# A graph layer on one core: more picks on the matrix engine, their index row read from PSUM, and a finer last group

## Chip, core and metric

The kernel runs on one NeuronCore of one Trainium2 chip. The metric is the device time of one execution in microseconds (us). The engines are named as in the profile: PE is TensorE (PEld its weight loads), DVE VectorE, ACT ScalarE, POOL GpSimd, SP the engine that only issues transfers here. Engines run their own streams and meet at semaphores.

## What is computed

The layer is a message-passing step of a graph network, with a residual and a layer norm behind it. 1,250 nodes have 128 features each, 20,000 edges have 50 features, a source, a destination (edges are sorted by destination) and a length.

```python
C = 0.5 * (cos(edge_length * (PI / CUTOFF)) + 1.0)
C = C * ((edge_length <= CUTOFF) & (edge_length >= 0.0))
h = gelu(edge_attr @ f_w0 + f_b0)
h = gelu(h @ f_w1 + f_b1)
h = gelu(h @ f_w2 + f_b2)
h = gelu(h @ f_w3 + f_b3)
xf = x @ lin1_w
msg = xf[src] * (h * C[:, None])
agg = segment_sum(msg, dst, num_segments=1250)
out = gelu(agg @ lin2_w + lin2_b) @ lin_w + lin_b
return layernorm(x + out)
```

## The kernel before

**Tiling.** The 20,000 edges are 160 tiles of 125; four tiles are a group (500 edges), two groups a pair, an even and an odd one. 20 pairs pass through a software pipeline. Nodes lie in ten chunks of 128. A loop over `passes` surrounds it all; for these inputs it runs once.

**The edge network.** PE makes layers 1 to 4 (`layer1` to `layer4`), ACT the gelus between them, and DVE adds the bias of layer 4 from PSUM (`add_bias4`, L666). Step p of the pipeline (function `pair` on each engine) makes layer 4 of pair p-1, layers 2 and 3 of pair p, layer 1 of pair p+1, and the messages and the scatter of pair p-2. Below, "the pair" of a message is q = p-2.

**Source rows.** `xf` is computed once (L433), copied from PSUM by ACT (L328) and written to DRAM. POOL then fetches `xf[src]` with one indirect DMA for each tile (L310), 125 rows of 512 bytes, in a fixed order, into eight slots of `gathered`. The gathers of a group wait only until the group eight before has been read. The two groups of pair 0 take another way (raw rows of x, L294, L493, L500).

**Picks.** For some pairs POOL leaves out the last tile of the odd group, and the rows are picked instead: DVE compares the tile's source numbers with the node numbers (`build_pick`, L710; ten chunks by 125 columns, a 0/1 matrix in bf16), PE multiplies this with `xf` split in three bf16 parts (`pick_rows`, L509, ten matmuls into bank `ps_pick`), and DVE sums the three parts into the free slot (L697). Before, this is done in 14 pairs (q mod 4 is 0, 1 or 2, without pair 0). The source numbers are broadcast to all 128 rows by a DMA from DRAM (875 KB) and cast by DVE (L729).

**Messages and scatter.** DVE builds the weighted one-hot of destinations (L675 hit, L677 onehot; both inputs in SBUF), multiplies h by the gathered rows (`message`, L682), and PE scatters four tiles of a group into a 64-column window (`scatter`, L483), which DVE adds to `aggT` (L719). A scatter waits for its whole group's message.

**End.** After the last scatter come `lin2` (L576), a gelu (ACT, L337), `lin` (L583) onto bias and residual that PE has put into PSUM earlier (`add_residual`, L516, L519), and the layer norm in three pieces of two, four and four chunks: statistics and the roots, then normalising on DVE (pieces 0 and 2, L776) and ACT (piece 1, L417), and the stores.

## Time and profile before

| what | value |
|---|---|
| median of 3 runs | 257.4 us (257.32 to 258.51) |
| profiled execution, its own time | 258.03 us |
| span from first to last instruction in it | 256.2 us |
| mean granted TensorE clock | 0.933 of 2.4 GHz |
| PE busy | 223.5 us (87%), 1130 instructions |
| DVE busy | 135.1 us (53%), 252 instructions |
| ACT busy | 110.0 us (43%), 181 instructions |
| POOL busy | 191.1 us (75%), 155 instructions |

The profile is of one execution; times in it count from its first instruction. "Busy" of POOL is the time in its gathers; between two of them the profile shows about 0.3 us of "issue", in which nothing is waited for. The profiled execution took 0.6 us more than the median.

### The profile page before, as it was taken

How to read it: one execution, taken by the hardware profiler on the slowest of the kernel's cores; microseconds unless marked ns; L12 is line 12 of the kernel's file. 1: busy time of each engine (PE TensorE's matmuls, PEld its weight loads, DVE VectorE, ACT ScalarE, POOL GpSimd, SP SyncE). 2: the span in 40 equal slices, each digit the busy share in tenths (PEclk: the TensorE clock that was granted, in tenths of full speed). 3: DMA queues.
4: the chain of work that ended last, by engine and by line, in shares of the span. 5: the costliest groups of instructions: out<-in, count | busy, mean ns of one | idle time of the engine just before them, and what ended most of it. 6: DMA issues, size and time to landing. Idle time of an engine off the chain costs nothing.

```text
span 256.2 us, 3892 instructions
## 1 busy us (share of the span) xinstructions
PE 223.5 (87%) x1130; PEld 148.6 (58%) x1130; DVE 135.1 (53%) x252; ACT 110.0 (43%) x181; POOL 191.1 (75%) x155
## 2 busy tenths in 40 slices
PE   3889999999799999899999599979968997898480
PEld 3535676765666766666766367555626565675350
DVE  5682186553666653666655356644424575613135
ACT  2457655354455364455365334515352453100052
POOL 6887888888888878888877888888778788887000
PEclk9999999999999999999999979989997999955587
DMA  6862222221221221221221212212121211111003
GB/s 209 248 202 72 75 74 46 70 75 46 66 72 42 70 74 41 72 72 41 69 75 41 75 37 72 72 36 72 47 72 40 72 31 43 41 45 45 10 0 101
DMA packets 17904, 17.70 MB, mean 69 GB/s; under 512 B 9244, under 2 KB 15183, under 8 KB 17894
## 3 DMA queue, kind: packets, MB, share of 16 engines
q0 software_dynamic: 11296, 9.52, 15.4%
q1 hardware_dynamic: 5872, 7.48, 9.6%
q10 hardware_dynamic: 726, 0.59, 0.8%
q8 instruction: 4, 0.07, 0.1%
q14 instruction: 6, 0.05, 0.0%
HBM read 16.14 MB, written 1.28 MB: 68 GB/s over the span
## 4 chain that ended last, share of the span: by engine, by line
POOL 53%; PE 21%; issue 15%; DVE 3%; ACT 2%; DMA 1%; POOLq 1%; ACTq 1%; another core or an unknown queue 1%; DVEq 1%
POOL gathered L310 53%; PE ps_agg L483 3%; PE ps_even L470 3%; PE ps_even L457 2%; PE ps_even L448 2%; PE ps_odd L457 2%; PE ps_even L462 2%; PE ps_odd L462 2%; PE ps_pick L509 1%; PE ps_odd L470 1%; DMA gathered<-xf_dram,src_idx 1%; PE ps_even L576 1%; DVE stats L762 1%; PE ps_odd L576 1%
## 5 line engine op out<-in xcount | busy, mean ns | idle before, releaser
L310 POOL DMA_INDIRECT gathered<-xf_dram,src_idx x138 | 180.4, 1307 | 42.1 <-issue 41.1
L483 PEld LDWEIGHTS ps_agg<-onehot,messages 125*128 125x128 f32 x320 | 43.8, 204 | 38.8 <-DVE messages L682 22.2
L483 PE MATMUL ps_agg<-onehot,messages 125*128 125x64 f32 x320 | 45.0, 287 | 17.8 <-DVE messages L682 15.9
L337 ACT ACTIVATE h<-ps_odd,biases_sb 128x500 f32<-128x500 f32 x61 | 41.3, 677 | 34.0 <-PE ps_odd L462 14.4
L337 ACT ACTIVATE h<-ps_even,biases_sb 128x500 f32<-128x500 f32 x61 | 40.9, 670 | 21.4 <-PE ps_even L462 9.7
L335 ACT ACTIVATE h<-pre 125x512 f32<-125x512 f32 x40 | 25.0, 626 | 51.8 <-DVE pre L666 43.4
L682 DVE TENSOR_TENSOR messages<-h,gathered 125x512 f32<-125x512 f32 x38 | 26.1, 690 | 32.5 <-DMA gathered<-xf_dram,src_idx 30.7
L470 PEld LDWEIGHTS ps_odd<-w_mlp_sb,h 128*125 128x125 f32 x160 | 21.3, 194 | 9.8 <-issue 9.8
L509 PE MATMUL ps_pick<-xf_parts,pick 128*125 128x384 bf16 x140 | 25.7, 331 | 0.0
L666 DVE TENSOR_TENSOR pre<-ps_odd,row_b_sb 125x512 f32<-125x512 f32 x20 | 13.8, 692 | 22.4 <-PE ps_odd L470 17.9
L509 PEld LDWEIGHTS ps_pick<-xf_parts,pick 128*125 128x125 bf16 x140 | 18.0, 136 | 12.5 <-issue 9.6
L457 PE MATMUL ps_even<-h,w_mlp_sb 128*128 128x500 f32 x40 | 23.0, 659 | 2.1 <-ACT h L337 2.1
L448 PE MATMUL ps_even<-edge_in,w_mlp_sb 50*128 50x500 f32 x42 | 24.1, 654 | 0.1
L470 PE MATMUL ps_even<-w_mlp_sb,h 128*125 128x128 f32 x160 | 24.1, 298 | 0.0
L448 PE MATMUL ps_odd<-edge_in,w_mlp_sb 50*128 50x500 f32 x42 | 24.1, 654 | 0.0
L666 DVE TENSOR_TENSOR pre<-ps_even,row_b_sb 125x512 f32<-125x512 f32 x20 | 13.8, 692 | 15.4 <-issue 10.6
L470 PEld LDWEIGHTS ps_even<-w_mlp_sb,h 128*125 128x125 f32 x160 | 21.0, 204 | 1.6 <-ACT h L337 1.6
L470 PE MATMUL ps_odd<-w_mlp_sb,h 128*125 128x128 f32 x160 | 21.3, 277 | 0.0
L462 PE MATMUL ps_odd<-h,w_mlp_sb 128*128 128x500 f32 x40 | 21.0, 607 | 0.0
L719 DVE TENSOR_TENSOR aggT<-aggT,ps_agg 128x64 f32 x40 | 8.9, 222 | 22.7 <-PE ps_agg L483 16.4
L457 PE MATMUL ps_odd<-h,w_mlp_sb 128*128 128x500 f32 x40 | 20.7, 599 | 0.0
L462 PE MATMUL ps_even<-h,w_mlp_sb 128*128 128x500 f32 x40 | 20.6, 595 | 0.0
(107 smaller groups left out, 184.5 us busy)
## 6 DMA issues: line engine op xcount, KB each, us to landing
edge_in<-in_edge_attrT SPq DMA_DIRECT2D x44, 97.7 KB
gathered<-xf_dram,src_idx POOLq DMA_INDIRECT x138
picked_i<-in_picked_src SPq DMA_DIRECT2D x1, 875.0 KB
xf_dram<-xf_sb SPq DMA_DIRECT2D x2, 256.0 KB
lin_xT_sb<-in_lin_xT SPq DMA_DIRECT2D x1, 369.0 KB
lin_xT_sb<-in_lin_xT SPq DMA_DIRECT2D x1, 320.0 KB, 3.1
w_mlp_sb<-in_w_mlp ACTq DMA_DIRECT2D x1, 256.0 KB
out<-normed SPq DMA_DIRECT2D x1, 256.0 KB
```

The costliest lines, as they stand in the source:

```text
L310: nc.gpsimd.indirect_dma_start(out=gathered[0:TILE, b, t, :], out_offset=None, in_=xf_dram[:, :], in_offset=bass.IndirectOffsetOnAxis(ap=s ...
L335: nc.scalar.activation(out_ap, in_ap, GELU).then_inc(done, 1)
L337: nc.scalar.activation(out_ap, in_ap, GELU, bias=biases_sb[:, layer:layer + 1]).then_inc(done, 1)
L448: nc.tensor.matmul(ps1[b][:, 0:GROUP], w0[b], edge_in[rows, slot, :], start=True, stop=True).then_inc(l1_done, 1)
L457: nc.tensor.matmul(ps23[b][:, 0:GROUP], w_mlp_sb[:, 1, :], h1[:, b, :], start=True, stop=True).then_inc(l2_done, 1)
L462: nc.tensor.matmul(ps23[b][:, 0:GROUP], w_mlp_sb[:, 2, :], h2[:, b, :], start=True, stop=True).then_inc(l3_done, 1)
L470: last = nc.tensor.matmul(ps4[b][0:TILE, t * FEAT:(t + 1) * FEAT], h3[:, b, t * TILE:(t + 1) * TILE], w_mlp_sb[:, 3, :], start=True, stop= ...
L483: last = nc.tensor.matmul(ps_agg[:, b * WINDOW:(b + 1) * WINDOW], messages[:, slot, t, :], onehot[:, p % 2, b * TILES_PER_GROUP + t, :], s ...
L509: last = nc.tensor.matmul(ps_pick[0:TILE, 0:3 * FEAT], pick[:, c, :], xf_parts[:, c, :, :].rearrange("p a f -> p (a f)"), start=(c == 0), ...
L666: nc.vector.tensor_tensor(pre4[:, (2 * p + b) % 4, :, :], ps4[b][0:TILE, :].rearrange("p (t f) -> p t f", f=FEAT), row_b3_sb[:, :].rearran ...
L682: nc.vector.tensor_tensor(messages[:, slot, :, :], h4[:, slot, :, :], rows_of_x, ALU.mult)\
L719: nc.vector.tensor_tensor(window, window, ps_agg[:, b * WINDOW:(b + 1) * WINDOW], ALU.add).then_inc(agg_added, 1)
```

## The change

1. A pick is made in every pair from 1 to 18 (18 picks instead of 14), so POOL issues 134 gathers instead of 138. The last pair has none.
2. The source numbers of the picks are no longer broadcast by DMA: one row of 9 KB is loaded on ACT's queue. For each pick PE spreads its 125 numbers over all partitions with a matmul of one row (`spread_pick_row`, `ones` x `picked_f`) into columns 384 to 508 of `ps_pick`, and DVE compares from there.
3. The split of `xf` in three parts is made from the PSUM banks, where the product still lies, instead of from its SBUF copy, in twelve smaller instructions, and stands earlier in DVE's order. PE waits for it ahead of the first layer 3.
4. ACT runs a gelu of one column behind the copies of `xf`, which brings the table load forward.
5. The very last group has a semaphore for each tile: four messages of a tile each, and each matmul of its scatter waits for its own.
6. The last four node chunks lie in two banks (`ps4[1]` and `ps_pick`), and their normalising is shared by DVE (two chunks) and ACT (two chunks).

Core of the diff:

```diff
-PICKED = (0, 1, 2)
+PICKS = PAIRS - 2
 def gathers_of(g):
-    return TILES_PER_GROUP - (g % 2 and is_picked(g // 2))
+    return TILES_PER_GROUP - (g % 2 and 0 < g // 2 < PAIRS - 1)
...
-            sp.wait_ge(xf_stored, 64)
-            sp.dma_start(picked_i[:, :, :].rearrange("p k e -> p (k e)"), picked_src.to_broadcast((ROWS, PICKS * TILE)))\
-                .then_inc(picked_loaded, 16)
...
+            act.dma_start(picked_i[:, :], picked_src).then_inc(picked_loaded, 16)
...
+            nc.scalar.activation(std[0:TILE, 0:1], half_pi[:, 0:1], GELU)
...
-                def pick_rows(before, turn, p):
-                    pe.wait_ge(parts_ready, 1)
-                    pe.wait_ge(pick_ready, r * PICKS + turn * len(PICKED) + picks_through(p))
+                def spread_pick_row(before, turn, p):
+                    pe.wait_ge(picked_cast, 1)
                     pe.wait_ge(message_done, before * (2 * TURN_PAIRS) + (2 * p + message_credit))
+                    nc.tensor.matmul(ps_pick[:, 3 * FEAT:3 * FEAT + TILE], ones[0:1, :],
+                                     picked_f[0:1, bass.ds(turn * (TURN_PAIRS * TILE) + (p - 1) * TILE, TILE)],
+                                     start=True, stop=True).then_inc(pick_row_done, 1)
+
+                def pick_rows(turn, p):
+                    pe.wait_ge(pick_ready, r * PICKS + turn * TURN_PAIRS + p)
...
                     layer3(before, p, 1)
                     if p >= 2:
+                        spread_pick_row(before, turn, p - 1)
                         scatter(before, p - 2, 1)
...
+                pe.wait_ge(parts_ready, 1)
                 layer3(first, 0, 0)
...
-                scatter(last, 3, 1)
+                scatter(last, 3, 1, by_tile=True)
...
+                def message_last(before):
+                    for t in range(TILES_PER_GROUP):
+                        if t == 0:
+                            dve.wait_ge(act4_done, before * (2 * TURN_PAIRS) + 2 * TURN_PAIRS)
+                        dve.wait_ge(last_landed[t], r * 16 + 16)
+                        ins = nc.vector.tensor_tensor(messages[:, 3, t, :], h4[:, 3, t, :],
+                                                      gathered[0:TILE, GATHER_SLOTS - 1, t, :], ALU.mult)
...
                 def build_pick(turn, p):
-                    row = picked_f[:, bass.ds(turn * len(PICKED) + (picks_through(p) - 1), 1), :]\
+                    dve.wait_ge(pick_row_done, r * PICKS + turn * TURN_PAIRS + p)
+                    row = ps_pick[:, 3 * FEAT:3 * FEAT + TILE].rearrange("p (o e) -> p o e", o=1)\
                         .to_broadcast((ROWS, NODE_CHUNKS, TILE))
```

PE, second half of a pipeline step (layer 3, the scatter of both groups). Before:

```order
L509 MATMUL ps_pick<-xf_parts,pick 125x384 x10
L462 MATMUL ps_even<-h,w_mlp_sb 128x500
L480 REGISTER_ALU
L483 MATMUL ps_agg<-onehot,messages 128x64 x4
L462 MATMUL ps_odd<-h,w_mlp_sb 128x500
L480 REGISTER_ALU
L483 MATMUL ps_agg<-onehot,messages 128x64 x4
```

and now:

```order
L518 MATMUL ps_pick<-xf_parts,pick 125x384 x10
L461 MATMUL ps_even<-h,w_mlp_sb 128x500
L480 REGISTER_ALU
L487 MATMUL ps_agg<-onehot,messages 128x64 x4
L461 MATMUL ps_odd<-h,w_mlp_sb 128x500
L510 REGISTER_ALU
L511 MATMUL ps_pick<-picked_f,ones 128x125
L487 MATMUL ps_agg<-onehot,messages 128x64 x4
```

The spreading matmul L511 stands between layer 3 and the scatter of the odd group; it waits for the same message as that scatter did.

DVE, the messages of a pair that had no pick before (q mod 4 is 3; `hit` to the next pick matrix). Before:

```order
L675 TENSOR_TENSOR hit<-dst_rel,iota_f 125x512
L676 REGISTER_ALU
L677 REGISTER_ALU
L677 TENSOR_TENSOR onehot<-hit,cut 125x512
L682 TENSOR_TENSOR messages<-h,gathered 125x512 x2
L710 ISA
L710 TENSOR_TENSOR pick<-picked_f,node_ids 128x1250
```

and now:

```order
L698 TENSOR_TENSOR hit<-dst_rel,iota_f 125x512
L699 REGISTER_ALU
L700 REGISTER_ALU
L700 TENSOR_TENSOR onehot<-hit,cut 125x512
L705 TENSOR_TENSOR messages<-h,gathered 125x512
L724 TENSOR_REDUCE gathered<-ps_pick 125x128
L713 ISA
L705 TENSOR_TENSOR messages<-h,gathered 125x512
L745 REGISTER_ALU
L749 TENSOR_TENSOR pick<-ps_pick,node_ids 128x1250
```

The sum of the picked rows stands between the two messages, as it did in the other pairs, and the compare L749 takes its first input from `ps_pick`.

DVE at the start, around the number of passes. Before, the split (L651 to L654) stood behind the tables; now it stands ahead of them:

```order
L642 CAST passes_i<-passes_f 1x1
L649 CAST xf_parts<-ps_even 128x4x128
L649 CAST xf_parts<-ps_odd 128x4x128
L649 CAST xf_parts<-ps_pick 128x2x128
L652 TENSOR_TENSOR ps_even<-ps_even,xf_parts 128x512
L652 TENSOR_TENSOR ps_odd<-ps_odd,xf_parts 128x512
L652 TENSOR_TENSOR ps_pick<-ps_pick,xf_parts 128x256
```

Six more of this kind follow, then the tables of destinations and weights and the cast of the 2,250 source numbers on one partition.

## Rows read from the trace of the kernel before

**Rows 1.** The page, part 4: engines' shares of the chain that ended last.
```profile
POOL 53%; PE 21%; issue 15%; DVE 3%; ACT 2%; DMA 1%; POOLq 1%; ACTq 1%; another core or an unknown queue 1%; DVEq 1%
```

**Rows 2.** Group of the gathers by line: xcount | busy us, mean ns | idle before <-releasers.
```profile
L310 POOL DMA_INDIRECT gathered<-xf_dram,src_idx x138 | 180.4, 1307 | 42.1 <-issue 41.1 <-DVE messages L682 0.9
```

**Rows 3.** Stretches: length, busy PE PEld DVE ACT POOL, PEclk, DMA share, GB/s.
```profile
66.00:134.00 68.00, 67.06 (x374) 45.33 (x374) 41.78 (x68) 34.13 (x56) 55.23 (x42) 1.00 0.24 61
134.00:220.00 86.00, 76.33 (x391) 50.46 (x391) 44.14 (x72) 35.56 (x59) 69.85 (x54) 0.94 0.21 54
226.00:246.00 20.00, 15.07 (x49) 11.28 (x49) 4.26 (x9) 0.83 (x2) 8.75 (x8) 0.51 0.11 28
246.00:253.00 7.00, 2.79 (x22) 2.35 (x20) 5.29 (x30) 4.58 (x10) 0.00 (x0) 0.96 0.02 7
```

**Rows 4.** Timeline (start, length, engine, line, tiles [idle before]): the first two and the last gather.
```profile
14.76 2.31 POOL L310 DMA_INDIRECT gathered<-xf_dram,src_idx  x1 [0.30 <-issue]
17.37 1.96 POOL L310 DMA_INDIRECT gathered<-xf_dram,src_idx  x1 [0.30 <-issue]
...
235.68 1.20 POOL L310 DMA_INDIRECT gathered<-xf_dram,src_idx  x1 [0.30 <-issue]
239.19 0.69 DVE L682 TENSOR_TENSOR messages<-h,gathered 125x512 f32<-125x512 f32 x1 [5.44 <-DMA gathered<-xf_dram,src_idx]
```

**Rows 5.** Timeline: a gather that starts inside a pick's compare.
```profile
205.04 1.46 DVE L710 TENSOR_TENSOR pick<-picked_f,node_ids 128x1250 bf16<-128x1250 f32 x1
205.11 2.45 POOL L310 DMA_INDIRECT gathered<-xf_dram,src_idx  x1 [0.30 <-issue]
```

**Rows 6.** Timeline: gathers that start inside other DVE products, PSUM or SBUF input.
```profile
34.52 0.69 DVE L682 TENSOR_TENSOR messages<-h,ps_agg 125x512 f32<-125x512 f32 x1 [0.97 <-PE ps_agg L500]
34.93 1.19 POOL L310 DMA_INDIRECT gathered<-xf_dram,src_idx  x1 [0.30 <-issue]
...
110.10 0.68 DVE L675 TENSOR_TENSOR hit<-dst_rel,iota_f 125x512 f32 x1
...
110.39 1.47 POOL L310 DMA_INDIRECT gathered<-xf_dram,src_idx  x1 [0.30 <-issue]
```

**Rows 7.** Timeline: three odd messages (pairs 6, 8, 9), PE between the last two.
```profile
94.95 0.69 DVE L682 TENSOR_TENSOR messages<-h,gathered 125x512 f32<-125x512 f32 x1 [0.28 <-DVE gathered L697]
...
113.98 0.69 DVE L682 TENSOR_TENSOR messages<-h,gathered 125x512 f32<-125x512 f32 x1 [0.27 <-DVE gathered L697]
...
116.36 1.09 PE L470 MATMUL ps_even<-w_mlp_sb,h 128*125 128x128 f32 x8
...
120.97 1.84 PE L509 MATMUL ps_pick<-xf_parts,pick 128*125 128x384 bf16 x10
...
123.60 0.69 DVE L682 TENSOR_TENSOR messages<-h,gathered 125x512 f32<-125x512 f32 x1 [0.19 <-DVE gathered L697]
```

**Rows 8.** Timeline: the start.
```profile
11.95 1.28 ACT L337 ACT_TABLE_LOAD   x1 [2.44 <-issue]
...
16.76 1.49 DVE L654 TENSOR_TENSOR xf_parts<-xf_rest,xf_parts 128x1280 bf16<-128x1280 f32 x1
...
18.36 1.10 PE L462 MATMUL ps_even<-h,w_mlp_sb 128*128 128x500 f32 x2
```

**Rows 9.** Timeline: the end, PE, ACT and DVE.
```profile
217.45 1.09 PE L470 MATMUL ps_even<-w_mlp_sb,h 128*125 128x128 f32 x8
...
220.96 0.69 PE L516 MATMUL ps_odd<-row_lin_b_sb,ones 1*128 1x256 f32 x2
...
239.94 1.97 PE L483 MATMUL ps_agg<-onehot,messages 125*128 125x64 f32 x8 [4.16 <-DVE messages L682]
...
242.67 1.22 PE L576 MATMUL ps_even<-aggT,w_node_sb 128*128 128x256 f32 x2 [0.76 <-DVE aggT L719]
...
246.59 0.69 ACT L337 ACTIVATE nodeT<-ps_even,biases_sb 128x512 f32<-128x512 f32 x1 [0.26 <-PE ps_even L576]
...
252.02 1.36 DVE L776 TENSOR_SCALAR normed<-ps_odd,mean_var,rstd 128x128 f32<-128x128 f32 x4
```

More of the change, by code:

```diff
@@ L420, in _ @@
             root(2)
-            act.wait_ge(normed_done[2], 1)
+            act.wait_ge(shift_done, 2)
+            c0, c1 = pieces[2]
+            for c in range((c0 + c1) // 2, c1):
+                last = nc.scalar.activation(normed[:, c, :], out_rows_of(c),
+                                            ACT.Identity, bias=shift[:, c:c + 1], scale=rstd[:, c:c + 1])
+            last.then_inc(normed_done[2], 1)
+            act.wait_ge(normed_done[2], 2)
             act.dma_start(out[FULL_CHUNKS * ROWS:NODES, :], normed[0:REST, FULL_CHUNKS, :]).then_inc(out_stored, 16)
@@ L582, in lin @@
                 for c in range(c0, c1):
[L583 removed]
+                    last = nc.tensor.matmul(out_rows_of(c),
                                             nodeT[:, c * ROWS:(c + 1) * ROWS], w_node_sb[:, 1, :],
[L585 removed]
+                                            start=False, stop=(c + 1 in [half[1] for half in halves]))
                 last.then_inc(node3_done, 1)
@@ L631, in _ @@
             nc.vector.tensor_copy(passes_i[:, :], passes_f[:, :]).then_inc(passes_ready, 1)
+            dve.wait_ge(xf_copied, 3)
+            xf_whole = [xf_bank[k][:, 0:(c1 - c0) * FEAT].rearrange("p (c f) -> p c f", f=FEAT)
+                        for k, (c0, c1) in enumerate(chunk_cuts)]
+            parts = [[xf_parts[:, c0:c1, part, :] for c0, c1 in chunk_cuts] for part in range(3)]
+            for k in range(3):
+                last = nc.vector.tensor_copy(parts[0][k], xf_whole[k])
+            chain(last)
+            for k in range(3):
+                last = nc.vector.tensor_tensor(xf_whole[k], xf_whole[k], parts[0][k], ALU.subtract)
+            chain(last)
+            for k in range(3):
+                last = nc.vector.tensor_copy(parts[1][k], xf_whole[k])
+            chain(last)
+            for k in range(3):
+                last = nc.vector.tensor_tensor(parts[2][k], xf_whole[k], parts[1][k], ALU.subtract)
+            last.then_inc(parts_ready, 1)
             chain(nc.vector.tensor_tensor(
@@ L790, in _ @@
             invert(2)
+            negate_mean(2)
             normalise(2)
```

132 lines of the change are left out of this document (68 added, 64 removed).

## The prediction, made before the changed kernel was run

> **What bounds the kernel now.** I read the chain that ended last first: over half of the span is POOL's gathers, and "issue", most of which stands between two gathers, is 15% [rows 1]. So the reader should see one engine that issues transfers from the beginning to the end. The groups by line then give the price of a gather: 138 gathers, 180.4 us busy and 42.1 us idle before them, of which only 0.9 us is a wait for a message [rows 2]. An undisturbed gather takes 1.19 us [rows 6]; with 42.1 / 138 = 0.305 us between two, the step is 1.495 us. At 1.19 us each, 138 gathers would be 164.2 us busy; the other 16.2 us is lengthening. With it POOL's time closes: the first gather starts at 14.76, 137 steps are 204.8, and 14.76 + 204.8 + 16.2 = 235.8, against 235.68 where the last one starts; its message starts 3.5 us later, at 239.19 [rows 4]. I call that moment T.
>
> PE is the second bound. From 66 to 134 us it is busy 67.06 of 68 us, from 134 to 220 only 76.33 of 86 [rows 3]: until about 134 the pairs run at PE's pace, then at POOL's. From one odd message to the next a PE-paced pair with a pick takes 123.60 - 113.98 = 9.6 us, 9.7 on average over several such pairs [rows 7]. Seven gathers take 7 x 1.495 = 10.5 us, so POOL, which has a head start, is slowly overtaken.
>
> **What lengthens a gather.** Rows 5 and 6 belong together. A gather that starts 0.07 us into a pick's compare takes 2.45 us: it ends 1.06 us after the compare [rows 5]. One that starts inside `hit`, which has two SBUF inputs, takes 1.47 us and ends 1.08 us after it; one that starts inside a message whose second input lies in PSUM takes 1.19 us, nothing more [rows 6]. I looked at each of the 138 in this way: 14 meet a compare and lose 10.4 us together, the first two meet the split of `xf` and lose 1.12 + 0.77 = 1.9 us [rows 4], 15 others lose 3.5 us together, a few tenths each, to `hit`, `onehot`, messages and a cast. Only the start of a gather is sensitive: a compare that begins 0.13 us or more after it costs nothing.
>
> The Trainium skill, page "SBUF — State Buffer", section "Summary: rules for kernel authors", says that a DVE instruction with two SBUF inputs contends with a GpSimd instruction that reads SBUF, and one with at most one SBUF input does not; the rows above agree. The same section also says, as inferred, that `tensor_tensor` does not stall descriptor generation, since that needs the write interface. By that sentence the compare's second input would not be what delays a gather, and moving it to PSUM would give nothing; the 2.45 us speaks against it, but I keep it as a rival (rival D).
>
> **The change part by part, at T.**
> (a) Four gathers less: 4 x 1.495 = 6.0 us off POOL's time.
> (b) The compare takes its row from PSUM, as the message at 34.52 did. The 10.4 us of 14 picks go, and the 18 picks cost POOL nothing. Bounds: all 10.4, or, if the delay stays, 10.4 / 14 x 18 = 13.4 in their place. I take the first, because rows 6 show the same kind of instruction at the same moment of a gather.
> (c) The split works from PSUM and is over before; its 1.9 us go. But the tables (of which some have two SBUF inputs) and a cast of 2,250 numbers now come behind it, at about 17 to 21 us, among the first gathers. Between 0 and 2 us; I take 1.0, since a cast of some 1.4 us covers the start of one gather almost surely.
> (d) The other meetings. Pair by pair `hit` and `onehot` cover 1.37 us of each 1.495 us step, so about one gather in each pair starts inside one of them and loses 0 to 0.6 us, 0.3 on average; the two messages stand in the step at nearly the same phases (1.4 and 3.8 us behind `hit`), so that they seldom cost a second time. Until now the compare pushed the gathers aside in each pair and left 3.5 us of this; without it I take 17 x 0.27 = 4.5 us, 1.0 more. Bounds: 0, and 10.5 us if the four products meet gathers independently (0.68 / 1.495 x 0.34 = 0.155 us each, 4 x 17 of them).
> T moves by -6.0 - 10.4 - 1.9 + 1.0 + 1.0 = -16.3 us, from 239.2 to 222.9.
>
> **PE's side.** Each spread adds one fp32 matmul of 125 columns with one row. The nearest row is the bias row of 256 columns, 0.69 us busy with its latency [rows 9]; four matmuls of 128 columns take 1.09 us [rows 7], 0.27 each. So 0.2 to 0.6 us, and I take 0.25: 18 x 0.25 = 4.5 us. It adds no wait on PE: it waits for the odd message, and the scatter queued right behind it waits for the same. What is new is on DVE: the compare can't start until layer 3 and the spread are through, about 1 us later than now, and the window sums and the next bias stand behind it. PE needs the matrix 4.6 us after a step begins (120.97 - 116.36 [rows 7]), so the cover is about 3.8 us; the next bias starts some 0.4 us later and its gelu has more slack than that. The four new picks are 1.8 us of PE each, but a step without a pick doesn't save as much now: pairs 7 (unpicked) and 8 together take 113.98 - 94.95 = 19.0 us, only 0.4 less than two picked ones [rows 7]. So I add 0.4 us for each. The table load of 1.28 us goes from the path ahead of the first gelu [rows 8]; the new wait for the split before layer 3 (now at 18.36, the split ends at 18.25) takes some of it back: I take 0.8 gained, between 0 and 1.3.
> The odd message of pair 9 is now at 123.60; it moves to 123.60 - 0.8 (start) + 9 x 0.25 (spreads) + 2 x 0.4 (picks of pairs 3 and 7) = 125.9. Eight pairs of 9.95 later comes that of pair 17, at 205.5, and 2 us later the tail. At full clock it is two layers 4 (1.8), a pick (1.8), bias and residual of ten chunks (5.8, by 0.69 for a bias and 0.22 to 0.35 for a chunk) and three scatters (2.5), 11.9 us: PE is ready for the last group at 219.4, which is 3.5 us ahead of T. So POOL still sets the end, and PE sets the pace until shortly before it. If POOL lost nothing at all in (c) and (d), T would be 217.4, and PE would be the bound at 219.4.
>
> **Behind T.** Now 256.2 - 239.2 = 17.0 us.
> (e) Message, scatter and the wait behind it: now 3.5 us from T to the start of `lin2` at 242.67, with a scatter of 1.97 us at the low clock [rows 9]. Then a quarter message (0.2), one matmul (0.2 to 0.5), the two window sums (0.6) and latencies: 1.4. -2.1 us.
> (f) The clock. The granted clock was about half (1.2 GHz) from 226 to 246 us, and nearly full from 246 on [rows 3]; before it fell PE had been busy only part of the time, waiting for messages. `lin2` took 242.67 to 246.59, 3.9 us [rows 9]; at 2.4 GHz it would be some 2.2. With PE busy up to 219.4 the low clock may come later or not at all. Between 0 and -1.7 (and +1 if `lin` falls into it as well); I take -1.0.
> (g) Normalising the last four chunks is 1.36 us on DVE [rows 9]; two chunks are 0.7, ACT's two end about 0.3 later. -0.4 us.
> Bias and residual in two banks add one matmul, hidden ahead of T.
>
> **Sum.** 256.2 - 16.3 - 2.1 - 1.0 - 0.4 = 236.4 us span. The profiled execution was 1.8 us longer than its span and 0.6 above the median, so 236.4 + 1.2 = 237.6 us.
>
> **Rivals.**
> A, the forecast: POOL sets the end, PE the pace; 234 to 240 us. 0.53.
> B: the gathers meet DVE's remaining products independently, now that DVE follows PE's pace and no compare realigns them: 10.5 instead of 4.5 us, 237.6 + 6.0 = 243.6. For it: 18 steps in which the phase wanders. Against: only 3.5 us now. 0.16.
> C: PE becomes the bound. A spread costs 0.55 us and not 0.25 (its operand address is computed anew each time, and its weights are another tile): 219.4 + 18 x 0.3 = 224.8, 1.9 above T, but the clock is then high behind it: 237.6 + 1.9 - 0.7 = 238.8. 0.12.
> D: the compare delays gathers from PSUM, too. T is 222.9 + 13.4 = 236.3; 237.6 + 13.4 = 251. Against it: 34.93 [rows 6]. 0.05.
> E: hardly any meeting, and a tail at full clock: T at PE's 219.4, so -3.5, and -0.7: 233.4. 0.10.
> F, slower than before: a compare with a row repeated from PSUM runs far slower than the 1.46 us of now, in the loop PE (spread), DVE (compare), PE (pick). The cover decides: beyond 1.46 + 3.8 = 5.3 us every further us is on PE's path 18 times. At 6.7 us, 219.4 + 18 x 1.4 = 244.6 is 21.7 us over T: 259. Messages from PSUM take 0.69 us as those from SBUF do, which speaks against it; a repeated row from PSUM is in no row. 0.03. What remains (0.01) is no difference.
>
> **Range and chances.** The likeliest case gives 237.6. From B's 243.6 down to E's 233.4 lie A, B, C and E, over 0.9; PE's start gained in full (0.5 less) moves the lower end to 232.8, and I leave the range at 232.8 to 243.8. Differences under 0.5% are about what a measurement of this kernel can't tell from none. Faster by more than 0.5%: A to E, 0.96. Same 0.01, slower 0.03.
>
> **What the changed profile would show.** 134 gathers with a mean of 1.22 to 1.25 us (now 1.307); none that starts inside a compare above 1.3 us; the compare still near 1.46 us; the last gather starting at about 219.4, with its message 3.5 us later; PE over 95% busy up to 200 us and a full clock there; `lin2` starting 1.4 us behind the last tile's message. I would be wrong if gathers inside compares still take 2 us (D), if the mean is 1.27 or more (B), or if PE has no idle time ahead of the last scatter (C, F).

## The result and the profile after

| | before | after |
| --- | --- | --- |
| device time, median | 257.95 us (4 runs, 257.32 to 261.54) | 250.64 us (4 runs, 248.47 to 250.86) |
| span of the profiled execution | 256.2 us | 248.9 us (250.74 us of device time) |
| PE busy | 223.5 us (87%), 1130 matmul instructions | 232.5 us (93%), 1208 matmul instructions |
| POOL busy | 191.1 us (75%) | 176.4 us (71%) |
| mean granted clock of PE | 0.933 | 0.954 |

The ratio of the times is 0.9705, with a 95% interval of 0.9632 to 0.9779: the change makes the kernel 3% faster. The prediction was 237.6 us, in a range of 232.8 to 243.8. The sign was right, the time was not: it came out 13.0 us above the forecast and outside the range. In the span the miss is 248.9 - 236.4 = 12.5 us, and the rest of this text accounts for those. Some executions of all these kernels are some us longer throughout, whatever the kernel; the times given below are those of the others (261.54 in the table is a long one), and where only a long one was profiled, single distances are read from it.

The first line is the chain that ended last of the kernel after, as in [rows 1]: it was 53% POOL, and it is 93% PE now. Two groups follow from the view by lines, the gathers (as in [rows 2]) and the compare.

```profile
PE 93%; DVE 2%; issue 2%; DMA 2%; ACT 0%; SPq 0%; DVEq 0%
```

```profile
L299 POOL DMA_INDIRECT gathered<-xf_dram,src_idx x134 | 166.1, 1240 | 41.0 <-issue 39.2 <-DVE messages L705 1.8
L749 DVE TENSOR_TENSOR pick<-ps_pick,node_ids 128x1250 bf16<-128x1250 f32 x18 | 26.3, 1460 | 28.4 <-PE ps_pick L511 17.0 <-issue 11.4
```

134 gathers with a mean of 1240 ns (1307 before) and a compare that still takes 1460 ns: POOL's side is what the prediction said. The stretches of the kernel after, in the columns of [rows 3], show where the time went instead:

```profile
66.00:134.00 68.00, 68.00 (x374) 45.58 (x373) 41.30 (x66) 31.24 (x52) 54.58 (x45) 1.00 0.25 63
134.00:220.00 86.00, 86.00 (x472) 57.29 (x470) 54.31 (x87) 40.27 (x66) 68.92 (x57) 1.00 0.23 59
220.00:240.00 20.00, 19.23 (x70) 14.21 (x69) 5.08 (x16) 2.32 (x4) 1.08 (x1) 0.57 0.02 6
```

PE, the second number behind the length, is busy 68.00 of 68 and 86.00 of 86 us. In [rows 3] it was busy 76.33 of 86 in the second stretch. It has no idle time at all up to the end of the pairs, and then it works at 0.57 of its clock. (Busy means here that an instruction was in PE; rows that overlap count once, so it doesn't say how densely columns were streamed.) These are the end of POOL's work, PE in the tail and DVE in the tail, in three pieces of the timeline of the kernel after:

```profile
219.44 1.64 POOL L299 DMA_INDIRECT gathered<-xf_dram,src_idx  x1 [0.31 <-issue]
```

```profile
222.22 1.66 PE L528 MATMUL ps_even<-ident,lin_xT_sb 128*128 128x128 f32 x8
223.67 1.81 PE L487 MATMUL ps_agg<-onehot,messages 125*128 125x64 f32 x8
...
229.87 3.51 PE L487 MATMUL ps_agg<-onehot,messages 125*128 125x64 f32 x16
234.15 1.22 PE L585 MATMUL ps_even<-aggT,w_node_sb 128*128 128x256 f32 x2 [0.77 <-DVE aggT L758]
```

```profile
228.10 0.89 DVE L737 TENSOR_TENSOR messages<-h,gathered 125x128 f32<-125x128 f32 x4
233.52 0.58 DVE L758 TENSOR_TENSOR aggT<-aggT,ps_agg 128x64 f32 x2 [4.53 <-PE ps_agg L487]
```

The last gather starts at 219.44. PE reaches the last group's scatter (the second half of the 16 matmuls at 229.87) only at about 231.6, when all four of its messages (228.10) are long written: DVE waits 4.53 us for PE, and nobody waits for a gather. A scatter of eight matmuls takes 1.81 us at 223.67; the same one takes 1.0 us in the pairs.

### The profile page after: what moved, and what is told of

The parts are those of the page before. It is cut to its first block, busy times and chain, and to the rows that moved or that the text cites. A ratio compares the mean times of both kernels' runs of the same rounds, so it can differ in the third digit from the quotient of the medians.

```text
span 248.9 us, 4074 instructions
## 1 busy us (share of the span) xinstructions
PE 232.5 (93%) x1208; PEld 155.5 (62%) x1208; DVE 145.3 (58%) x270; ACT 111.0 (45%) x184; POOL 176.4 (71%) x151
## 4 chain that ended last, share of the span: by engine, by line
PE 93%; DVE 2%; issue 2%; DMA 2%; ACT 0%; SPq 0%; DVEq 0%
PE ps_agg L487 16%; PE ps_pick L518 13%; PE ps_even L447 9%; PE ps_even L469 7%; PE ps_odd L461 7%; PE ps_even L461 7%; PE ps_odd L469 7%; PE ps_even L456 7%; PE ps_odd L456 7%; PE ps_pick L511 3%; DMA lin_xT_sb<-in_lin_xT 2%; PE ps_even L585 1%; PE ps_even L432 1%; PE ps_odd L528 1%; PE ps_odd L525 1%
## 5 line engine op out<-in xcount | busy, mean ns | idle before, releaser
L299 POOL DMA_INDIRECT gathered<-xf_dram,src_idx x134 | 166.1, 1240 | 41.0 <-issue 39.2
L330 ACT ACTIVATE h<-ps_even,biases_sb 128x500 f32<-128x500 f32 x61 | 40.8, 669 | 28.3 <-issue 13.7
L487 PEld LDWEIGHTS ps_agg<-onehot,messages 125*128 125x128 f32 x320 | 42.7, 202 | 10.6 <-issue 8.4
L487 PE MATMUL ps_agg<-onehot,messages 125*128 125x64 f32 x320 | 44.4, 285 | 0.0
L749 DVE TENSOR_TENSOR pick<-ps_pick,node_ids 128x1250 bf16<-128x1250 f32 x18 | 26.3, 1460 | 28.4 <-PE ps_pick L511 17.0
L518 PEld LDWEIGHTS ps_pick<-xf_parts,pick 128*125 128x125 bf16 x180 | 23.1, 136 | 16.3 <-issue 12.6
L518 PE MATMUL ps_pick<-xf_parts,pick 128*125 128x384 bf16 x180 | 33.1, 331 | 0.0
L469 PEld LDWEIGHTS ps_odd<-w_mlp_sb,h 128*125 128x125 f32 x160 | 20.5, 188 | 8.7 <-issue 8.7
L461 PE MATMUL ps_even<-h,w_mlp_sb 128*128 128x500 f32 x40 | 21.0, 607 | 2.1 <-issue 2.1
L461 PE MATMUL ps_odd<-h,w_mlp_sb 128*128 128x500 f32 x40 | 21.9, 630 | 0.0
L469 PE MATMUL ps_even<-w_mlp_sb,h 128*125 128x128 f32 x160 | 21.9, 280 | 0.0
L456 PE MATMUL ps_even<-h,w_mlp_sb 128*128 128x500 f32 x40 | 20.2, 586 | 1.0 <-issue 1.0
L469 PE MATMUL ps_odd<-w_mlp_sb,h 128*125 128x128 f32 x160 | 20.7, 273 | 0.0
L469 PEld LDWEIGHTS ps_even<-w_mlp_sb,h 128*125 128x125 f32 x160 | 19.3, 189 | 1.8 <-issue 1.0
L724 DVE TENSOR_REDUCE gathered<-ps_pick 125x128 f32<-125x384 f32 x18 | 10.0, 557 | 15.6 <-PE ps_pick L518 9.9
```

The lines of the kernel that those rows point to most:

```text
L299: nc.gpsimd.indirect_dma_start(out=gathered[0:TILE, b, t, :], out_offset=None, in_=xf_dram[:, :], in_offset=bass.IndirectOffsetOnAxis(ap=s ...
L330: nc.scalar.activation(out_ap, in_ap, GELU, bias=biases_sb[:, layer:layer + 1]).then_inc(done, 1)
L456: nc.tensor.matmul(ps23[b][:, 0:GROUP], w_mlp_sb[:, 1, :], h1[:, b, :], start=True, stop=True).then_inc(l2_done, 1)
L461: nc.tensor.matmul(ps23[b][:, 0:GROUP], w_mlp_sb[:, 2, :], h2[:, b, :], start=True, stop=True).then_inc(l3_done, 1)
L469: last = nc.tensor.matmul(ps4[b][0:TILE, t * FEAT:(t + 1) * FEAT], h3[:, b, t * TILE:(t + 1) * TILE], w_mlp_sb[:, 3, :], start=True, stop= ...
L487: last = nc.tensor.matmul(ps_agg[:, b * WINDOW:(b + 1) * WINDOW], messages[:, slot, t, :], onehot[:, p % 2, b * TILES_PER_GROUP + t, :], s ...
```

## The experiments

The working theory after this trace had three parts. First, a spread costs PE 0.6 us and not 0.25, because its operands have one row and stand between matmuls with full operands. Second, PE's new wait for the split delays the start. Third, the tail runs at 1.2 GHz although PE is never idle in it. The rivals were that a spread costs so much by its place or its columns, that the compare in PSUM or its later start is what holds the pairs, and that gathers set the end after all.

### The spread with operands of 128 rows

The stationary operand `ones` and the moving one `picked_f` get 128 rows. All rows of `picked_f` but the first are zero, so the sum is the same.

```diff
-        ones = sb("ones", [GROUPS, ROWS])
+        ones = sb("ones", [ROWS, ROWS])
-        picked_f = sb("picked_f", [1, PICKS * TILE])
+        picked_f = sb("picked_f", [ROWS, PICKS * TILE])
...
-                    nc.tensor.matmul(ps_pick[:, 3 * FEAT:3 * FEAT + TILE], ones[0:1, :],
-                                     picked_f[0:1, bass.ds(...)],
+                    nc.tensor.matmul(ps_pick[:, 3 * FEAT:3 * FEAT + TILE], ones[:, :],
+                                     picked_f[:, bass.ds(...)],
...
+            chain(nc.vector.memset(picked_f[:, :], 0.0))
-            nc.vector.tensor_copy(picked_f[:, :], picked_i[:, :]).then_inc(picked_cast, 1)
+            nc.vector.tensor_copy(picked_f[0:1, :], picked_i[:, :]).then_inc(picked_cast, 1)
```

> The spreading matmul gets an operand of 128 rows (127 of them zero) instead of one row; everything else is the changed kernel. Theory S (a spread costs 0.61 us of PE's step, of which only some 0.2 us is its own columns, the rest the change between a one-row operand and full ones): the step falls from 10.31 to about 9.95 us, 18 x 0.36 = 6.5 us less, 244 to 245 us, PE still the bound. Rival (the cost is the wait for the message and the register work ahead of the spread, whatever its operand): step 10.3, 250.7 us.

Measured: 242.26 us (242.14 and 242.38), a ratio to before of 0.9386 (0.9281 to 0.9492), 8.4 us less than the changed kernel. PE around the spread, from the timeline, first of the changed kernel and then of this one:

```profile
109.86 1.06 PE L461 MATMUL ps_odd<-h,w_mlp_sb 128*128 128x500 f32 x2
110.85 0.48 PE L511 MATMUL ps_pick<-picked_f,ones 1*128 x2
111.26 1.10 PE L487 MATMUL ps_agg<-onehot,messages 125*128 125x64 f32 x8
112.20 1.09 PE L469 MATMUL ps_even<-w_mlp_sb,h 128*125 128x128 f32 x8
```

```profile
204.51 1.06 PE L461 MATMUL ps_odd<-h,w_mlp_sb 128*128 128x500 f32 x2
205.40 0.38 PE L511 MATMUL ps_pick<-picked_f,ones 128*128 x2
205.62 1.01 PE L487 MATMUL ps_agg<-onehot,messages 125*128 125x64 f32 x8
206.46 1.09 PE L469 MATMUL ps_even<-w_mlp_sb,h 128*125 128x128 f32 x8
```

The busy times overlap, so the reader should take starts. From the start of L461 to that of L469 it is 2.34 us with one row and 1.95 us with 128. The same stretch without a spread is 1.74 us in the trace of before:

```profile
114.62 1.06 PE L462 MATMUL ps_odd<-h,w_mlp_sb 128*128 128x500 f32 x2
115.52 1.00 PE L483 MATMUL ps_agg<-onehot,messages 125*128 125x64 f32 x8
116.36 1.09 PE L470 MATMUL ps_even<-w_mlp_sb,h 128*125 128x128 f32 x8
```

So a spread of one row costs 0.60 us and one of 128 rows 0.21 us. The other 0.39 us lies in the one-row matmul and on both sides of it: the one before it takes 0.99 instead of 0.89 us until the next starts, the spread 0.41 instead of 0.22, and the scatter behind it 0.94 instead of 0.84. The step from one odd message to the next goes from 10.31 to 9.92 us, on average over the 16 from pair 1 to pair 17. Over these 16 it is 6.2 us; another 2.3 us of the difference at pair 17 (212.21 against 203.78) was there at pair 1 already and comes from the start, which scatters (below). The expectation had the step right and the whole time 2 us too high, since it left out the start.

With this one edit the two bounds meet. POOL, PE and DVE at the end, from the timeline of this kernel:

```profile
220.44 1.20 POOL L299 DMA_INDIRECT gathered<-xf_dram,src_idx  x1 [0.30 <-issue]
```

```profile
221.33 3.52 PE L487 MATMUL ps_agg<-onehot,messages 125*128 125x64 f32 x16
223.74 0.29 DVE L738 TENSOR_TENSOR messages<-h,gathered 125x128 f32<-125x128 f32 x1 [1.12 <-DMA gathered<-xf_dram,src_idx]
```

The last tile's message waits for its gather and is written at 224.03. But PE doesn't wait for it: its 16 matmuls run without a pause, and the two of the last tile start at 224.2. So neither engine alone is the bound there; the chain that ended last is 59% PE and 21% POOL, whose gathers stand at its end. `lin2` starts at 225.97, 5.5 us behind the last gather's start. The forecast said 4.9.

### Every spread issued twice

If 0.2 us of the 0.6 are the spread's own columns and 0.4 the change of shape, then a second one of the same shape, right behind the first, must cost 0.2 us.

```diff
                                      start=True, stop=True)
+                    nc.tensor.matmul(ps_pick[:, 3 * FEAT:3 * FEAT + TILE], ones[0:1, :],
+                                     picked_f[0:1, bass.ds(...)], start=True, stop=True)
```

> Each spread is issued twice, one behind the other, into the same columns. Theory S: the second one costs its columns alone, 0.2 us, 18 x 0.2 = 3.7 us more, 254 to 255 us, step 10.5. Rival (each one-row matmul costs the whole 0.6 us): 11 us more, 261.7 us, step 10.9.

Measured: 249.55 us, in one execution; the expected 3.7 us more don't show in it. The profiled execution has a span of 254.9 us, so I read single starts from its timeline:

```profile
113.50 1.06 PE L461 MATMUL ps_odd<-h,w_mlp_sb 128*128 128x500 f32 x2
114.49 0.48 PE L511 MATMUL ps_pick<-picked_f,ones 1*128 x2
114.81 0.38 PE L514 MATMUL ps_pick<-picked_f,ones 1*128 x2
115.12 1.10 PE L487 MATMUL ps_agg<-onehot,messages 125*128 125x64 f32 x8
```

From L461 to L487 it is 1.62 us, where one spread takes 1.40 (109.86 to 111.26 above): the second costs 0.22 us, and the step grows by 0.22 us, to 10.53. That settles the split of the price, by the timeline and not by the whole time. What makes the switch dear was not separated further. The Trainium skill, page "TensorEngine Tiling (Array Packing)", section "Key Properties", says that changing the tiling mode drains TensorE; the extra time on both sides of the one-row matmul fits that. Whether a one-row operand is such a change, and the drain itself, no run here shows.

### The split of `xf` back behind the tables

The split works from the SBUF copy again, behind the tables, and PE's wait for it stands ahead of the first pick instead of ahead of the first layer 3.

```diff
                 next_layer1(first, 0)
-                pe.wait_ge(parts_ready, 1)
                 layer3(first, 0, 0)
...
+            dve.wait_ge(xf_copied, 3)
+            chain(nc.vector.tensor_copy(xf_parts[:, :, 0, :], xf_sb[:, :, :]))
+            chain(nc.vector.tensor_tensor(xf_rest[:, :, :], xf_sb[:, :, :], xf_parts[:, :, 0, :], ALU.subtract))
```

> The split of xf is made from its SBUF copy behind the tables again, PE waits for it only at the first pick. Theory W (PE's wait of 2.1 us for the split, and the stretch at 1.2 GHz behind it, cost 2 us of PE's path): the odd message of pair 1 comes at about 45.3 instead of 47.3 us, 248 to 249 us in all; the two first gathers lengthen again by some 2 us, which costs nothing as POOL isn't the bound. Rival (the end is set by POOL): 252 us.

Measured: 247.37 us (247.12 and 247.62), a ratio to before of 0.9584 (0.9475 to 0.9694). PE's start, from the timeline of the changed kernel, with the end of the split on DVE between, and then of this one:

```profile
12.68 1.10 PE L456 MATMUL ps_even<-h,w_mlp_sb 128*128 128x500 f32 x2 [1.01 <-issue]
...
17.31 0.41 DVE L658 TENSOR_TENSOR xf_parts<-ps_pick,xf_parts 128x256 bf16<-128x256 f32 x1
```

```profile
17.78 1.95 PE L461 MATMUL ps_even<-h,w_mlp_sb 128*128 128x500 f32 x2 [2.13 <-issue]
```

```profile
12.64 1.10 PE L457 MATMUL ps_even<-h,w_mlp_sb 128*128 128x500 f32 x2 [1.24 <-ACT h L331]
...
15.55 1.11 PE L462 MATMUL ps_even<-h,w_mlp_sb 128*128 128x500 f32 x2
```

Both start layer 2 at 12.6 to 12.7 us at the full clock. From there to layer 3 it is 5.10 us with the wait and 2.91 without: the wait costs 2.2 us. Behind it layer 3 takes 1.95 us instead of 1.11, since the granted clock fell just as the wait ended (at 17.9); until the next layer 4 this is another 1.4 us. The odd message of pair 1 came at 47.30 and comes at 43.66 now, 3.6 us earlier, and from pair 17 to the end both take the same 36.7 us. So all that this edit moves is the start, and by more than the expected 2 us, which had left out part of the low clock's price.

### The row broadcast by DMA and compared from SBUF

18 picks as in the changed kernel, but the source numbers come as before: broadcast, cast on all partitions, and the compare has two SBUF inputs. No spreads.

```diff
-                    row = ps_pick[:, 3 * FEAT:3 * FEAT + TILE].rearrange("p (o e) -> p o e", o=1)\
+                    row = picked_f[:, bass.ds(turn * TURN_PAIRS + (p - 1), 1), :]\
```

> 18 picks, but their source numbers are broadcast by DMA and compared from SBUF as before; no spreads. Theory (a compare with two SBUF inputs delays a gather by 0.74 us, one from PSUM does not): the gathers' mean rises from 1.240 to about 1.34 us, the last one starts at about 232 instead of 219.4, PE (11 us less to do) waits for it, 250 to 253 us in all. Rival (what delayed the gathers before was something else than the compare's second SBUF input): last gather at 220, PE bound at 240 us.

Measured: 250.02 us (249.12 and 250.93), a ratio of 0.9687 (0.9551 to 0.9824), as slow as the changed kernel, for another reason. The gathers by line, and a gather that starts inside a compare, from the timeline:

```profile
L303 POOL DMA_INDIRECT gathered<-xf_dram,src_idx x134 | 173.5, 1295 | 43.1 <-issue 42.2 <-DVE messages L698 0.9
```

```profile
209.59 1.46 DVE L741 TENSOR_TENSOR pick<-picked_f,node_ids 128x1250 bf16<-128x1250 f32 x1
...
209.98 2.14 POOL L303 DMA_INDIRECT gathered<-xf_dram,src_idx  x1 [0.30 <-issue]
```

The gather ends 1.07 us after the compare, as the one in [rows 5] did (1.06). The gathers are 7.4 us longer together than in the changed kernel, and the last one starts at 228.87 instead of 219.44. In the kernel with operands of 128 rows a gather that starts 0.71 us into a compare with its row in PSUM takes 1.18 us:

```profile
205.82 1.46 DVE L750 TENSOR_TENSOR pick<-ps_pick,node_ids 128x1250 bf16<-128x1250 f32 x1 [1.35 <-PE ps_pick L511]
206.53 1.18 POOL L299 DMA_INDIRECT gathered<-xf_dram,src_idx  x1 [0.30 <-issue]
```

This holds for all of them: of the 16 gathers that start inside a compare here, 15 end 1.05 to 1.07 us after it (the other starts at its very end), while none of the 18 in the changed kernel, nor of the 18 in the one with 128 rows, takes more than 1.20 us. So the compare's second SBUF input is what delays a gather, and not, as the inferred sentence behind rival D would have it, something else. The pairs give the spread's price once more: from pair 1 to pair 9 PE sets the pace here too, and a step takes 9.70 us without a spread against 10.31 with it, 0.61 us. The move to PSUM is worth its matmul, if that has full operands: this kernel without any spread is 7.8 us slower than the one with them (250.02 against 242.26).

### Useless matmuls in PE's tail

The changed kernel, with seven repetitions of a layer 2 product (500 columns, into a bank whose content nobody reads any more) among the tail's small matmuls.

```diff
+                def filler():
+                    nc.tensor.matmul(ps1[0][:, 0:GROUP], w_mlp_sb[:, 1, :], h1[:, 0, :], start=True, stop=True)
...
+                filler()
                 pick_rows(LAST_TURN, 2)
                 add_residual(0)
+                filler()
                 scatter(last, 2, 0)
                 add_residual(1)
+                filler()
                 scatter(last, 2, 1)
                 add_residual(2)
                 add_residual(3)
+                filler()
                 scatter(last, 3, 0)
+                filler()
                 scatter(last, 3, 1, by_tile=True)
```

Two more stand inside the last scatter.

> The changed kernel with seven matmuls more in PE's tail, each like layer 2 (500 columns, 128 rows) into a bank that nobody reads: work that does nothing. Theory K (PE, though never idle there, runs its last 11 us and lin2 at 1.2 GHz, which costs 5 to 8 us of the path, because what it does there is small): the granted clock stays high to the end of the scatter, 7 x 0.84 = 5.9 us more work, 5.3 + 2 us less, so 249 to 250 us, lin2 2.9 instead of 4.7 us long. Rival (the low clock comes at that place whatever PE does): 250.7 + 5.9 or, at the low clock, + 11.7, 257 to 262 us.

First the clock in the changed kernel's tail, in short stretches, and then in this kernel's, from its tail's start to `lin2` and through it (columns as in [rows 3]):

```profile
222.00:223.00 1.00, 1.00 (x6) 0.79 (x6) 0.00 (x0) 0.00 (x0) 0.00 (x0) 0.85 0.16 52
223.00:224.00 1.00, 1.00 (x8) 1.00 (x6) 0.00 (x0) 0.00 (x0) 0.00 (x0) 0.50 0.00 0
```

```profile
215.40:236.80 21.40, 20.68 (x112) 14.16 (x110) 9.83 (x21) 1.90 (x3) 5.80 (x5) 1.00 0.07 17
236.80:241.00 4.20, 4.16 (x24) 3.15 (x25) 1.11 (x6) 2.85 (x4) 0.00 (x0) 1.00 0.00 0
```

Measured: the clock stays at 2.4 GHz through the whole tail and `lin2`. In the changed kernel it falls to 1.2 GHz at 222.7, with PE busy 1.00 of 1.00 us during and after the fall. What PE does there are biases of one row, residual products of 128 columns with the identity, and scatters of 64 columns. The tail from its first layer 4 to `lin2` takes 19.58 us (217.26 to 236.84) against 18.87 (215.28 to 234.15), with 7 x 0.84 = 5.9 us of useless work in it: without that it would be 13.7, so the low clock costs 5.2 us there. From `lin2` to the end it is 12.0 instead of 14.75 us. From the odd message of pair 17 to the end it is 34.7 us instead of 36.7. The first row of `lin2` in this timeline (its like of the changed kernel, 1.22 us at 234.15, stands above):

```profile
236.84 0.70 PE L596 MATMUL ps_even<-aggT,w_node_sb 128*128 128x256 f32 x2 [0.76 <-DVE aggT L769]
```

In the whole time the 2.0 us don't show: 248.56 us (247.0 to 250.67), on another chip and without a ratio to before, and with an odd message of pair 1 at 48.59, 1.3 us later than in the changed kernel's trace. What is shown is the tail alone.

The other traces bear it out. In eight profiled executions with PE at or near the bound and no useless matmul in the tail, the clock falls 9.4 to 12.7 us behind the odd message of pair 17 (10.5 in the changed kernel); in the two kernels with seven such matmuls (this one and one below) it holds for 29 and 31 us, until `lin2` and `lin` are over.

The Trainium skill, page "TensorE: Matmul & The Clock Gate", Part 1, lets the clock fall after idle time. The fall at the start, right behind the wait of 2.13 us, agrees with it; the one at 222.7 doesn't, since the profile has no idle time of PE there, and the measurement decides: here work of this kind didn't keep the clock, and a few wide matmuls among it did. Which of the three kinds lets it fall was not separated.

### Both repairs together, without and with the useless matmuls

The operands of 128 rows and the old split, and then the same with the seven useless matmuls, on one chip.

```diff
-                                     picked_f[0:1, bass.ds(...)],
+                                     picked_f[:, bass.ds(...)],
...
-                pe.wait_ge(parts_ready, 1)
                 layer3(first, 0, 0)
```

> The 128-row operand of the spread and the split from SBUF behind the tables together. Theory (with the 128-row operand POOL's last gather plus 3.5 us sets the end, as the forecast had it, and PE arrives just then): the 1.9 us that PE gains at the start are not seen at the end, last gather at 220 to 221, 241.5 to 243 us. Rival (PE still is the bound): 240 us.

> e6 with the seven filling matmuls of e5. Theory K: they lie in time in which PE would wait for gathers, the clock stays high, lin2 takes 2.9 instead of 4.7 us and the last tile's scatter 0.2 us less: 2 to 3 us less than e6, 239 to 240 us. Rival (low clock there in any case): the filling costs its time at 1.2 GHz, 244 to 247 us.

Measured: 242.47 and 245.38 us without, 243.79 (243.2 to 245.93) with. With the operands of 128 rows alone it was 242.26, on another chip, and on this one the kernel of before scattered too much for a ratio. So the old split shows no gain on top, but these runs don't tell why. In both profiled executions PE came late to the second bank of `xf` (at 8.39 and 7.64 us, against 6.96 in the changed kernel), and the clock had not risen when layer 2 came (layer 1 ahead of it already takes 1.04 us a matmul, where it takes 0.58 at the full clock; layer 2 takes 2.04 us for a pair of matmuls at 14.55 and 13.79), so that the start lost again what the missing wait had gained, with odd messages of pair 1 at 48.55 and 47.85. And PE, not POOL, set the end of the kernel without the useless matmuls (90% of its chain):

```profile
225.79 3.52 PE L488 MATMUL ps_agg<-onehot,messages 125*128 125x64 f32 x16
226.79 0.29 DVE L729 TENSOR_TENSOR messages<-h,gathered 125x128 f32<-125x128 f32 x1 [1.18 <-DMA gathered<-xf_dram,src_idx]
```

The last message is written at 227.1, and PE comes to its tile at 228.7. The expectation that PE would arrive just then was not put to the test, since PE's start was late. With the useless matmuls the way from pair 17 to the end is 34.3 us (208.23 to 242.5) and without 37.1 (207.99 to 245.1), but seven are too many once POOL is near:

```profile
228.50 1.06 PE L479 MATMUL ps_even<-h,w_mlp_sb 128*128 128x500 f32 x2
229.40 0.33 PE L493 MATMUL ps_agg<-onehot,messages 125*128 125x64 f32 x2
```

In this timeline the last tile's scatter (229.40) stands behind a useless matmul, while its message started at 227.44. PE comes some 1.6 us late by its own doing. `lin2` (230.49) runs at the full clock, 0.70 us for its first two matmuls.

### Four useless matmuls, all ahead of the last pair's scatter

```diff
                 scatter(last, 3, 0)
-                filler()
                 scatter(last, 3, 1, by_tile=True)
```

The two inside the last scatter are left out, too.

> The kernel of e7 with four of the seven filling matmuls, those ahead of the last pair's scatter; the three behind it, one of which stood ahead of the last tile's matmul and made PE late by 1.6 us, are left out. If the clock holds for the 4 to 5 us that remain: lin2 1.5 us earlier behind the last gather than in e7 (5.1 instead of 6.6 us), 1.5 us less, 240 to 242 us. Rival (the clock falls again ahead of lin2): lin2 4.6 us long, no gain over e6.

Measured: 241.35 and 242.22 us, the lowest of all that were run; the ratio to before is 0.9353 (0.9283 to 0.9422). Against the 242.26 of the operands of 128 rows alone this is no difference that these runs can tell. From the timeline (its span is 243.3 us):

```profile
226.73 0.43 PE L491 MATMUL ps_agg<-onehot,messages 125*128 125x64 f32 x2 [1.50 <-DVE messages L737]
228.61 1.22 PE L594 MATMUL ps_even<-aggT,w_node_sb 128*128 128x256 f32 x2 [1.45 <-DVE aggT L758]
```

PE now waits for the last tile (1.50 us) and for the sums (1.45 us), and the clock is down when `lin2` starts (1.22 us for its first two matmuls, 0.70 at the full clock). So the rival came, though the time lies in the expected range: in this execution useless work that ended ahead of the waits didn't carry the clock over them.

### The last group undivided

The operands of 128 rows, and the last group's message and scatter in one piece each.

```diff
-                scatter(last, 3, 1, by_tile=True)
+                scatter(last, 3, 1)
```

> The kernel of e1 (128-row operand), with the last group's message and scatter undivided as in the kernel before. Term (e) of the forecast, 2.1 us less by the division: 242.3 + 1.5 to 2.5, 244 to 245 us, with lin2 about 3.5 us behind the start of the last message. Rival (the division brings nothing because PE is late there anyway): 242.3 us.

Measured: 247.6 us (245.91 to 248.58). `lin2` starts 8.7 us behind the last gather's start, against 5.5 us in the divided kernel. That looks like a gain of 3.2 us for the division, but the traces forbid this reading. From this kernel's timeline:

```profile
225.58 3.52 PE L487 MATMUL ps_agg<-onehot,messages 125*128 125x64 f32 x16
```

```profile
224.72 0.69 DVE L706 TENSOR_TENSOR messages<-h,gathered 125x512 f32<-125x512 f32 x1 [0.82 <-DMA gathered<-xf_dram,src_idx]
```

The last message is there at 225.4, and PE begins the last pair's two scatters only at 225.58, and then runs through both without a pause. PE was the bound in this execution (its odd message of pair 17 is at 208.13, 4.4 us later than in the divided kernel's), and a divided message would have given nothing. Neither expectation is met, and what the division is worth is left open.

### The old split without the early table load

```diff
-            nc.scalar.activation(std[0:TILE, 0:1], half_pi[:, 0:1], GELU)
```

> The kernel of e3 (split from SBUF, behind the tables) without the small gelu that brings the table load forward (part 4 of the change undone). It says what the table load was worth to PE's start: e3 had the odd message of pair 1 at 43.66 us. Theory: the load's 1.3 us and the low clock behind the longer wait (1.2 us more for two layers) come back, 46.0 to 46.5 us, in all 249.5 to 250.5 us. Rival (only the load's own 1.3 us): 45.0 us, 248.7 us in all.

Measured: 251.4 us (249.11 to 252.22), against 247.37 of the same kernel with it, on another chip. The start, from the timeline:

```profile
14.19 1.81 PE L455 MATMUL ps_even<-h,w_mlp_sb 128*128 128x500 f32 x2 [2.11 <-issue]
```

Layer 2 starts 1.55 us later (14.19 against 12.64), and the clock falls as it begins (1.81 us against 1.10), which costs another 1.5 us until layer 1 of the next pair (17.59, against 14.51). The odd message of pair 1 comes at 46.86, 3.2 us later. About 1.0 us of this is not the edit's, since `xf` itself was ready that much later in this execution. So the load alone is worth some 0.6 us, and the clock 1.5 more where it falls for it; it can fall there with the early load, too, as in the kernel with operands of 128 rows (layer 2 at 12.63 takes 2.00 us, behind a wait of 1.14).

### The changed kernel once more

On the chip of the kernel before and of the one with four useless matmuls, with no edit, to see how its start and its time scatter.

> The changed kernel as it is, for the same chip as the others of this call: 248.5 to 251 us, step 10.31 us.

Measured: 249.99 and 247.88 us, a ratio of 0.9629 (0.9548 to 0.971). One row of its timeline:

```profile
18.16 1.10 PE L461 MATMUL ps_even<-h,w_mlp_sb 128*128 128x500 f32 x2 [2.25 <-issue]
```

The wait for the split is there again (2.25 us), but the clock did not fall behind it, and the odd message of pair 1 came at 46.18, 1.1 us earlier. The wait is a property of the change; whether the clock falls behind it is not decided the same way in every execution.

## Why the prediction was wrong

**Right.** The bound of before, and all of POOL's side. Terms (a) to (d) put the start of the last gather at 219.4, and it is 219.44. To the last 0.1 us this is luck: in the same kernel's other profiled execution it is 221.60. The shares behind it were off, too. In the trace of before 11 gathers start inside a compare and lose 9.2 us, not 14 with 10.4, and 16 others lose 4.6 us, not 15 with 3.5; in the changed one the lengthening that is left is 6.6 us, not 5.5, and the first gather starts 0.3 us earlier. The gathers' mean was to be 1.22 to 1.25 us and is 1.240. No compare delays a gather any more: rival D (251 us) fell, although its time was close to the measured one. The right number for the wrong reason can be told apart only in the trace, and the kernel that compares from SBUF shows what D would have looked like. The compare from PSUM takes 1.46 us, so rival F fell as well. B's 10.5 us of random meetings didn't come. The two picks added up to pair 9, for which I took 0.8 us, cost nothing on PE: eight steps from pair 1 to pair 9 take 82.45 us (47.30 to 129.75) against 77.74 before (45.86 to 123.60), and the spreads alone are 8 x 0.61 = 4.9 us, all of the difference. What the prediction puts into the section "Summary: rules for kernel authors", that an instruction with at most one SBUF input doesn't contend and the inferred sentence, stands in the section "Who interferes with whom" of the same page.

**Wrong: the step that made PE ready at 219.4.** It was ready at 231.6. Four of its terms failed in the same direction, and the one for the picks, 1.0 us too high up to pair 17, in the other:

- The spread. I took 0.25 us, from four full matmuls of 128 columns, out of bounds of 0.2 to 0.6. It is 0.60, or 0.61 by the step. The row that spoke for the upper bound was the only one with one row (the bias of 256 columns, 0.69 us [rows 9]), and I set it aside. 17 spreads of 0.36 more are 6.1 us up to pair 17.
- The start. I took 0.8 us gained, by placing the split's end of 18.25 beside a layer 3 that starts at 18.36 in before [rows 8]. But the early table load moves layer 2 forward, and the wait holds what would have followed it. Together with the fallen clock the start lost 0.8 us (the odd message of pair 1 at 47.30 against 45.86, of which 0.61 is the first spread): 1.6 us off the forecast. With the spreads' 6.1 and less the 1.0 us for picks, pair 17 is 6.7 us late (212.21 against 205.5).
- The way from there to the tail is 3.07 us, not 2 (+1.1): a spread is in it, and I had rounded down.
- The tail. I took 11.9 us "at full clock". It took 16.3 (+4.4), because the clock fell at 222.7. The sum itself was right: in the kernel with useless matmuls the same way takes 15.2 us at the full clock, of which 4 x 0.84 = 3.4 are theirs, which leaves 11.9.

6.7 + 1.1 + 4.4 = 12.2 us; 219.4 + 12.2 = 231.6.

**Wrong: term (f), the clock behind the gathers.** I took 1.0 us of gain, with the reason that PE had been busy only part of the time before the clock fell [rows 3]. I had put the fall down to idle time, which the trace of before could not tell from the kind of work. Idle time does go with some falls: in the pairs of before it fell three times (at 146.7, 170.6 and 194.5), each time within 1.3 us of the end of a wait of PE of 1.4 to 3.5 us. But with PE busy all the time it fell all the same, and more work lies in it now: `lin2` takes 4.7 us (234.15 to 238.82), not the 2.9 of the forecast, and the first part of `lin` is at the low clock too. From `lin2` to the end it is 14.75 us instead of 12.1, 2.65 more.

The sum of both: PE at 231.6 and 2.55 us to `lin2` give 234.15, where the forecast had 222.9 + 1.4 = 224.3, so 9.85 us; with the 2.65 behind it 12.5 us, the whole miss.

**Terms (e) and (g).** (e) can't be read in the changed kernel, where PE is late for all four tiles; in the kernel with operands of 128 rows it is 5.5 us from the last gather's start to `lin2` against 7.0 before, 1.5 us instead of 2.1, at the low clock. Counted as the forecast did, from the last message, it is 2.2 us (223.74 to 225.97) and not 1.4. That kernel also shows what is left of the miss once the spread is repaired: its span is 240.6 us, 4.2 above the 236.4, of which 1.7 lie ahead of `lin2` (225.97 against 224.3) and 2.5 behind it, where the clock is low. (g): from the last gelu of `nodeT` to the end of the normalising on DVE it is 6.75 us (238.82 to 245.57), against 6.79 before [rows 9], though `lin` began at the low clock now. The gain of 0.4 may have gone there; no run shows it.

**The rival that was right and too small.** C had the mechanism (a spread of 0.55 us makes PE the bound) and gave 238.8, because it counted a full clock behind T and nothing for the start, and because it held PE's other terms to be exact. The uncertainties of PE's side lay all on one side of a slack of 3.5 us. The range took C's price of the spread in, but not that price together with a slower tail.

## What to carry to other kernels

When a change takes work off the bounding engine, cost the second engine as carefully as the first, at both ends of each of its prices together: here a slack of 3.5 us over 220 carried the whole gain. A matmul whose operands have one row, between matmuls with full ones, is not priced by its columns: fill the operand with zeros to the full number of rows and measure the step. A stretch that was read at the full clock must not be forecast at it elsewhere, if other work stands there: look at what PE does in it, not only at whether it is busy.

## What the runs showed of the hardware

- A spread of one row and 125 columns costs 0.60 us among full matmuls and 0.21 us with 128 rows; a second one-row matmul behind the first costs 0.22 us.
- The clock fell from 2.4 to 1.2 GHz at 222.7 us with PE busy 1.00 of every 1.00 us, in biases of one row, products of 128 columns with the identity and scatters of 64. Among them seven useless matmuls of 500 columns held it at 2.4 GHz, and with 5.9 us more work the way from pair 17 to the end became 2.0 us shorter.
- An indirect gather that starts inside a compare with two SBUF inputs ends 1.07 us after it (2.14 us long); inside one whose row lies in PSUM it takes 1.18 us, and never more than 1.20 in 18 cases. The compare takes 1.46 us in both cases.
